# Cross-attention of a fused decoder in one pass over the scores: exponentials by queries kept, scaled, turned and copied out

## The reference

```python
q, k, v = x1 @ Wq, *split(x2 @ Wkv)              # 16 heads of 64, 256 queries, 256 keys
attn = softmax(einsum('bhid,bhjd->bhij', q, k) * 64 ** -0.5)
out = einsum('bhij,bhjd->bhid', attn, v) @ Wo + bo
```

## Time and profile before

| | |
|---|---|
| median of 3 runs | 3820.13 us (3819.62 to 3820.35) |
| span of the profiled execution | 3818.7 us |
| PE busy | 3224.1 us (84%) |
| DVE busy | 2835.6 us (74%) |
| ACT busy | 2082.8 us (55%) |
| POOL busy | 922.9 us (24%) |
| mean granted PE clock | 0.941 of full speed |

### The profile page before, as it was taken

One profiled execution on the slowest core, in us unless ns is written; L12 is line 12 of the kernel. 1 busy time (PEld: TensorE's weight loads), 2 busy tenths in 40 slices (PEclk: granted clock), 3 DMA queues, 4 the chain that ended last, 5 costly groups with the idle time before them and its releaser, 6 DMA issues.

```text
span 3818.7 us, 59008 instructions
## 1 busy us (share of the span) xinstructions
PE 3224.1 (84%) x22354; PEld 2240.1 (59%) x22402; DVE 2835.6 (74%) x4915; ACT 2082.8 (55%) x4816; POOL 922.9 (24%) x740
## 2 busy tenths in 40 slices
PE   2568989898898989989898998989889898988877
PEld 1245656666565666656566665656656565665655
DVE  4687786868778687877868778786877868687622
ACT  3356655565665656566464655656566565555432
POOL 1423050221404122140411305031230503114000
PEclk8679999999999999999999999999999999999988
DMA  5212141422304142130413213041331404123110
GB/s 187 79 61 92 31 137 47 145 70 79 128 23 148 51 136 78 55 127 33 163 51 127 87 43 138 34 158 57 114 100 31 150 34 152 62 99 109 48 42 17
DMA packets 205692, 336.50 MB, mean 88 GB/s; under 512 B 23968, under 2 KB 175008, under 8 KB 190688
## 3 DMA queue, kind: packets, MB, share of 16 engines
q1 hardware_dynamic: 205408, 332.72, 25.6%
HBM read 311.66 MB, written 20.97 MB: 87 GB/s over the span
## 4 chain that ended last, share of the span: by engine, by line
PE 55%; DVE 23%; ACT 15%; issue 6%; POOL 0%; SPq 0%; DMA 0%; DVEq 0%; ACTq 0%
PE ps L880 7%; PE ps L628 6%; PE ps L609 5%; PE ps L941 4%; DVE nm L1559 3%; PE ps L795 3%; PE ps L781 3%; PE ps L771 3%; PE ps L826 2%; ACT ps L1062 2%; PE ps L640 2%; DVE region_x L1536 2%; PE ps L553 2%; ACT region_y L1211 2%; PE ps L670 2%
## 5 line engine op out<-in xcount | busy, mean ns | idle before, releaser
L1323 POOL TENSOR_TENSOR region_x<-region_x 128x512 f32<-128x512 f32 x512 | 646.8, 1275 | 360.4 <-DVE region_x L1536 359.2
L1536 DVE TENSOR_TENSOR_SCAN region_x<-ps,region_x 128x512 f32<-128x512 f32 x512 | 614.2, 1213 | 76.4 <-ACT ps L1062 76.3
L1062 ACT ACTIVATE ps<-region_x,aneg 128x255 f32<-128x255 f32 x1024 | 440.0, 474 | 326.3 <-DVE region_x L1536 324.1
L1303 POOL TENSOR_TENSOR region_x<-region_x 128x512 f32<-128x512 f32 x96 | 121.7, 1267 | 1195.2 <-ACT region_x L1010 1190.2
L1315 POOL TENSOR_TENSOR region_x<-region_x 128x512 f32<-128x512 f32 x128 | 162.8, 1272 | 1021.4 <-DVE region_x L1516 881.2
L1559 DVE TENSOR_REDUCE nm<-ps 128x4 f32<-128x1024 f32 x256 | 308.0, 1221 | 62.5 <-PE ps L609 56.7
L880 PE MATMUL ps<-xTy,wide 128*128 128x256 f32 x1280 | 331.2, 410 | 1.1 <-DVE region_y L1723 1.1
L1211 ACT ACTIVATE region_y<-ps,rmax 128x256 f32<-128x256 f32 x512 | 235.8, 497 | 126.0 <-DVE rmax L1664 126.0
L880 PEld LDWEIGHTS ps<-xTy,wide 128*128 128x128 f32 x1280 | 251.8, 203 | 47.4 <-issue 8.7
L1664 DVE TENSOR_REDUCE rmax<-ps 128x4 f32<-128x1024 f32 x128 | 152.3, 1220 | 151.2 <-PE ps L807 151.2
L1516 DVE TENSOR_TENSOR region_x<-region_x,ps 128x512 f32<-128x512 f32 x384 | 255.0, 664 | 5.9 <-PE ps L553 5.0
(11 more groups left out here) (249 smaller groups left out, 6884.6 us busy)
## 6 DMA issues: line engine op xcount, KB each, us to landing
region_x<-rows_of_dt SPq DMA_DIRECT2D x1024, 128.0 KB, 2.9
wide<-in_wgate SPq DMA_DIRECT2D x16, 1280.0 KB, 8.2
wide<-in_wup SPq DMA_DIRECT2D x16, 1280.0 KB, 10.9
down<-in_wmoe SPq DMA_DIRECT2D x16, 1280.0 KB, 7.4
wide<-in_wq SPq DMA_DIRECT2D x16, 1024.0 KB, 5.4
wide<-in_wk SPq DMA_DIRECT2D x16, 1024.0 KB, 7.3
wide<-in_wv SPq DMA_DIRECT2D x16, 1024.0 KB, 9.6
down<-in_wo SPq DMA_DIRECT2D x16, 1024.0 KB, 12.5
```

What stands on the lines that cost most here:

```text
L1062: last = f(ps[:, 1 + 2 * (k % 2), half * T + 1:(half + 1) * T], dt_rep[k % SLOTS][:, 1:T], ACT.Exp, scale=aneg[:, k, half:half + 1])
L1323: nc.gpsimd.tensor_tensor(hbuf[k % HSLOTS], hbuf[k % HSLOTS], csb, ALU.mult).then_inc(hc_ready, 1)
L1536: nc.vector.tensor_tensor_scan(flat(hbuf[k % HSLOTS]), ps[:, 1 + 2 * (k % 2), :], flat(hbuf[k % HSLOTS]), 0.0, ALU.mult, ALU.add).then_inc ...
```

## The change

There is one pass. PE makes the scores of a pair by queries, always in banks 5 and 6. DVE takes the maximum of each head by itself. ACT takes the exponentials of a head into one of four slots `PQ`, which are kept, and their sums. DVE takes the reciprocal of the two sums and scales the head's two tiles in place. PE turns the head with four 128x128 f32 transposes into bank 7, ACT copies it into one of two slots `PT64`, and PE multiplies by the values as before. The second scores, the logarithm and the shift are gone. The orders of all four engines are new.

Names of the pieces of y below: s(u) scores of a pair, m(u) its maxima, E(u) its exponentials, S(n) the scaling of a head, T(n) its turning, C(n) its copy (with o(j): the copy of two pairs' outputs), pv(u) a pair's product with the values. Of x: l. is latent attention (l.s scores, l.m maxima, l.sT second scores, l.e exponentials, l.w weighting, l.pv values, l.o copy, l.oT, l.on, l.OT, l.On turning, scaling and copying of the result, l.wo the output projection, l.res its residual sum), win the input projection of the next sequence, conv its products, g1 to g3 the norms' estimates. The new orders of the attention stage, with x's pieces in brackets:

```diff
--- before.py
+++ after.py
@@ -38,15 +38,16 @@
 ORDER = {
-    "sp": (123, ...), "pe": (60, ...), "act": (80, ...), "v": (141, ...)
+    "sp": (140, ...), "pe": (61, ...), "act": (84, ...), "v": (145, ...)
 }
@@ -94,7 +95,7 @@
 END_STEPS = 5
 DIGIT_STEPS = 8
 DT_STEPS = 6
-Y_STEPS = 38
+Y_STEPS = 50
 A_STEPS = 5
 AY_STEPS = 3
 
@@ -152,8 +153,6 @@
         mask = sb("mask", (P, TT, T), BF16)
         VP0, VP1 = sb("VP0", (P, TT, VW)), sb("VP1", (P, TT, VW))
         nm0, nm1 = sb("nm0", (P, TT, P)), sb("nm1", (P, TT, P))
-        shiftb = sb("shiftb", (P, TT, P), BF16)
-        shiftT = sb("shiftT", (P, T), BF16)
         rmax = sb("rmax", (P, TT, 2, 8))
         rsum = sb("rsum", (P, TT, 2, 8))
         route = sb("route", (P, 5, TT, E))
@@ -212,9 +211,9 @@
         
         QT2, KT2, VV = in_y(0, (8, T)), in_y(2048, (8, T)), in_y(4096, (TT, 1024))
         OT2 = QT2
-        WSLOTS = 6
-        PT64 = in_y(6144, (WSLOTS, TT, T))
-        junk2 = in_y(6144, (8, T))
+        QSLOTS, WSLOTS = 4, 2
+        PQ = in_y(6144, (QSLOTS, TT, T))
+        PT64 = in_y(6144 + QSLOTS * TT * T, (WSLOTS, TT, T))
         mhT, sg, t1, rcmp = in_y(0, (KM, T)), in_y(2560, (2, 2, T)), in_y(3584, (2, 2, T)), in_y(4608, (2, TT, E, E))
 
         wst, wst2, hmv1 = in_y(0, (KD, FF)), in_y(2048, (KD, FF)), in_y(4096, (D,))
@@ -288,7 +287,7 @@
                     self.on_ps, self.oT = sem(tag + "_on_ps"), sem(tag + "_oT")
                 else:
                     self.kevac, self.rsum = sem(tag + "_kevac"), sem(tag + "_rsum")
-                    self.ln, self.shift = sem(tag + "_ln"), sem(tag + "_shift")
+                    self.scaled = sem(tag + "_scaled")
                 if masked:
                     self.weighed = sem(tag + "_weighed")
                 self.proj = sem(tag + "_proj")
@@ -795,40 +794,26 @@
                             last = mm(bank(b)[:, t % 2, :], wq2[:, k, t * P:(t + 1) * P], xTy[:, k, :],
                                       start=(k == 0), stop=(k == KD - 1))
                     last.then_inc(a.proj, 1)
-                yield
-                pe.wait_ge(a.evac, at(i, 4, 4))
-                for u in range(8):
-                    yield
-                    if u >= 2:
-                        pe.wait_ge(a.rsum, at(i, 8, u - 1))
+
+                def scores(u):
+                    if u:
+                        pe.wait_ge(a.rsum, at(i, 16, 2 * u))
                     for qt in range(TT):
                         for g in range(2):
                             r = slice(64 * g, 64 * g + 64)
-                            last = mm(ps[:, a.pair_bank(u) + g, qt * T:(qt + 1) * T], QT2[r, u, qt * P:(qt + 1) * P],
+                            last = mm(ps[:, 5 + g, qt * T:(qt + 1) * T], QT2[r, u, qt * P:(qt + 1) * P],
                                       KT2[r, u, :], start=True, stop=True)
                     last.then_inc(a.s_ps, 1)
-                yield
-                pe.wait_ge(a.shift, i + 1)
-                turned_shift = ps[:, 4, 0:P].bitcast(BF16)
-                for qt in range(TT):
-                    last = tr(turned_shift[:, qt * P:(qt + 1) * P], shiftb[:, qt, :], W["identb"][:])
-                last.then_inc(a.shift_ps, 1)
-                yield
-                pe.wait_ge(a.shifted, i + 1)
-
-                def scores(n):
-                    t = n // 2
-                    both = [(slice(64 * g, 64 * g + 64), a.sT_bank(n + g)) for g in range(2)]
-                    if n >= 2:
-                        pe.wait_ge(a.probs, at(i, 16, n - 1))
+
+                def turned(n):
+                    pe.wait_ge(a.scaled, at(i, 16, n + 1))
+                    if n:
+                        pe.wait_ge(a.probs, at(i, 16, n))
                     for kt in range(TT):
-                        for r, b in both:
-                            mm(ps[:, b, kt * T:(kt + 1) * T], KT2[r, t, kt * P:(kt + 1) * P], QT2[r, t, :],
-                               start=True, stop=False)
-                        for r, b in both:
-                            last = mm(ps[:, b, kt * T:(kt + 1) * T], W["selx"][r, t, :], shiftT[r, :], start=False, stop=True)
-                            if kt == TT - 1:
-                                last.then_inc(a.sT_ps, 1)
+                        for qt in range(TT):
+                            last = tr(ps[:, 7, kt * T + qt * P:kt * T + (qt + 1) * P],
+                                      PQ[:, n % QSLOTS, qt, kt * P:(kt + 1) * P], W["ident"][:])
+                    last.then_inc(a.sT_ps, 1)
 
                 def times_v(t):
                     pe.wait_ge(a.probs, at(i, 16, 2 * t + 2))
@@ -842,14 +827,23 @@
                                       start=(kt == 0), stop=(kt == TT - 1))
                     last.then_inc(a.pv, 1)
 
-                for n in range(0, 16, 2):
-                    yield
-                    scores(n)
-                    if n >= 4:
-                        yield
-                        times_v(n // 2 - 2)
-                yield
-                times_v(6)
+                yield
+                pe.wait_ge(a.evac, at(i, 4, 4))
+                scores(0)
+                for u in range(9):
+                    yield
+                    if u:
+                        turned(2 * u - 2)
+                    yield
+                    if u >= 2:
+                        times_v(u - 2)
+                    yield
+                    if u + 1 < 8:
+                        scores(u + 1)
+                    yield
+                    if u:
+                        turned(2 * u - 1)
+                yield
                 times_v(7)
                 yield
                 pe.wait_ge(down_cross, at(i, 16, 16))
@@ -1200,35 +1194,34 @@
                     act.wait_ge(a.pv, at(i, 8, 2 * j + 2))
                     f(OT2[:, 2 * j:2 * j + 2, :], bank(4), ACT.Copy).then_inc(a.o, 1)
 
-                for u in range(8):
-                    yield
+                def exps(u):
                     table(EXP_LN)
-                    act.wait_ge(a.rmax, at(i, 8, u + 1))
-                    if u >= 2:
-                        act.wait_ge(a.rsum, at(i, 8, u - 1))
-                    for qt in range(TT):
-                        for g in range(2):
-                            last = f(junk2[:, 4 * (u % 2) + 2 * qt + g], ps[:, a.pair_bank(u) + g, qt * T:(qt + 1) * T], ACT.Exp,
+                    for g in range(2):
+                        n = 2 * u + g
+                        act.wait_ge(a.rmax, at(i, 16, n + 1))
+                        if n >= QSLOTS:
+                            act.wait_ge(a.sT_ps, at(i, 16, n - QSLOTS + 1))
+                        for qt in range(TT):
+                            last = f(PQ[:, n % QSLOTS, qt, :], ps[:, 5 + g, qt * T:(qt + 1) * T], ACT.Exp,
                                      bias=rmax[:, qt, g, u:u + 1], accum_out=rsum[:, qt, g, u:u + 1])
-                    last.then_inc(a.rsum, 1)
-                yield
-                table(EXP_LN)
-                act.wait_ge(a.rsum, at(i, 8, 8))
-                f(rsum[:], rsum[:], ACT.Ln).then_inc(a.ln, 1)
-                yield
-                act.wait_ge(a.shift_ps, i + 1)
-                f(shiftT[:], ps[:, 4, 0:P].bitcast(BF16), ACT.Copy).then_inc(a.shifted, 1)
-                for n in range(16):
-                    yield
-                    table(EXP_LN)
+                        last.then_inc(a.rsum, 1)
+
+                def turned(n):
                     act.wait_ge(a.sT_ps, at(i, 16, n + 1))
-                    if n >= WSLOTS and n % 2 == 0:
+                    if n >= WSLOTS:
                         act.wait_ge(a.pv, at(i, 8, (n - WSLOTS) // 2 + 1))
-                    f(PT64[:, n % WSLOTS].rearrange("p k q -> p (k q)"), ps[:, a.sT_bank(n), :], ACT.Exp).then_inc(a.probs, 1)
-                    if n >= 9 and n % 4 == 1:
-                        output(n // 4 - 2)
-                yield
-                output(2)
+                    f(PT64[:, n % WSLOTS].rearrange("p k q -> p (k q)"), ps[:, 7, :], ACT.Copy).then_inc(a.probs, 1)
+
+                for u in range(9):
+                    yield
+                    if u < 8:
+                        exps(u)
+                    for n in (2 * u - 2, 2 * u - 1):
+                        yield
+                        if u:
+                            turned(n)
+                    if u >= 3 and u % 2 == 1:
+                        output(u // 2 - 1)
                 yield
                 output(3)
                 yield
@@ -1367,9 +1360,9 @@
             for k in range(TAPS - 1):
                 nc.vector.memset(taps[k][:, :, 0:TAPS - 1 - k], 0.0).then_inc(setup_v, 1)
             n += 3
-            for buf, value in ((VP0, 1.0), (VP1, 1.0), (nm0, 0.0), (nm1, 0.0), (shiftb, 0.0), (wsplit, 0.0)):
+            for buf, value in ((VP0, 1.0), (VP1, 1.0), (nm0, 0.0), (nm1, 0.0), (wsplit, 0.0)):
                 nc.vector.memset(buf[:], value).then_inc(setup_v, 1)
-            v.wait_ge(setup_v, n + 10)
```

(38 more changed lines are left out.)

8 lines of the change are left out of this document (4 added, 4 removed), and 19 rows, old and new, of the table ORDER.

## The result

The changed kernel takes 3938.0 us (median of 4 runs, 3927.7 to 3954.3) against 3820.2 for the kernel before on the same chip: ratio 1.0309, 95% interval [1.0289, 1.0328]. Slower was right; 3872 was not, the loss is 118 us and not 52. The profiled execution has a span of 3925.2 us, 106.5 more than in the earlier trace rows.

The account below looks back on a forecast made before the run. No engine is full over the period, so stages decide: PE's stream bounds the attention stage, which closes with a serial stretch. 15 sequences x 4 - 8 = +52 us gives 3871 profiled, 3872 as median; range 3775 to 3940.

Parts of the forecast that it names:

- the scan stage: From the MoE's end to the next cross scores: gain up to 2.2, late rows up to +1, taken as 0.
- Attention, +4: Attention stage of each sequence with a partner: +4 us, taken between PE's bound and the full walk.
- PE's work alone (+2.5): Attention stage counting only PE's added and removed work, without waits: +2.5 us a sequence.
- the walk (+5.1): Attention stage followed piece by piece through the engines' queues, each wait charged in full: +5.1 us a sequence.
- step 2: From turning the latent shift to the latent output projection: with some 3 us idle PE, projection 4.1 us later.
- Rival D: Transposes in the attention stage take a record's full 280 ns each: +9 us a sequence, 4015; chance 0.02.
- MoE, 0 (bounds -2.6 and +1): MoE: fewer ACT table changes against PE's waits at the dt projections; the pair costed at 0.
- The dt projections: Two projections now ahead of an up-projection on PE, which waits there for ACT; costed within the pair at 0.
- rival C: Gaps on PE lower its clock in the attention stage: +7 to +9 a sequence, 120 in all, 3940; chance 0.11.
- Last sequence, -8: Last sequence, without a partner, from first cross scores to wo2: -8 us, bounds -16 and 0.
- The sum: Whole kernel: 15 sequences with a partner at +4 and the last at -8, +52 us, giving 3872.

Follow-up runs that it names:

- the run at 3830: Changed kernel with SP's issue order of the kernel before put back, cross weights behind half of row 11; 3830.2 us, ratio 1.0021.
- the first run: Changed kernel with only SP's issue order put back to that of the kernel before; 3830.2 us, ratio 1.0021.
- the entry, twice: Changed kernel, self-attention's start freed: MoE's closing sum ahead of the scan's products on DVE, 3939.0 us; then ACT's copy ahead of the decays too, 3967.6 us.

## Why the prediction was wrong

*The step that failed* is the scan stage: "That gains up to 2.2 if the rows of dt are there. But SP now issues the 3 MB of cross weights between the first two rows of dt and the next, so the second product can wait for them, and the closing sum stands behind it: up to +1. I take 0." The place and the first wait are right, the size is not. The order gains 3.3 with rows on time, and the rows take 5.6 from it: 83.1 to 88.7, +2.3 against the kernel before. I priced one wait, of DVE's second product, at up to 1 us. It is 4.26 in the sequence shown; and I left out that every row behind the weights is late, so that GpSimd's second product waits too, y0 behind it, and self-attention's keys behind y0. The price stood in the trace of before, where the last rows of a sequence are issued behind the same 3 MB and wo2: a row landed 2.8 us after its issue ahead of them and 12.5 behind them (2059 to 2073.3 us, then 2075.2 to 2078.5):

```profile
region_x<-rows_of_dt SPq DMA_DIRECT2D x15, 128.0 KB, 2.8
...
region_x<-rows_of_dt SPq DMA_DIRECT2D x3, 128.0 KB, 12.5
```

The prediction named this zero as one that could fail, and the loss between the MoE's end and the self-attention scores as its sign.

*Attention, +4.* With SP's order put back it is +2.6 up to the projection, and 0 behind it. The sum is that of PE's work alone (+2.5), not of the walk (+5.1), but in part by chance: PE's bound put 1.5 ahead of the projection and 1.0 behind it. The prediction took a transpose at 0.137 us; over the run at 3830 it occupied 0.164 (168.2 / 1024). For the nine heads in step 2 that is 36 x 0.027 = 1.0 more, and with it the bound of that step comes to the measured start. PE stayed full, since other pieces of x stand between those of a head; the doubled transposes and scores show that added work of PE lengthens the stage. Behind the projection the estimate of the third norm stands where the walk put it, 10.3 us on, but the end of wo2 doesn't move.
A row of four transposes took 0.60 to 0.66 us, and a further transpose 0.123. Rival D, 0.28 each, would have shown as 18 us a sequence in the run with transposes twice, which was 6.3.
The Trainium skill (TensorE: Matmul & The Clock Gate, Part 4: PE-mode transpose) gives about 275 ns in a kernel. The trace agrees for a record's own length (288 to 292 ns) and disagrees for what it occupies.

*MoE, 0 (bounds -2.6 and +1).* It is +1.8, beyond the bound. With SP's order put back it is +1.0: PE waits 2.0 for the masks ahead of the second down product, a wait I didn't list. The dt projections, which I did list, cost 0.5. The other 0.8 in the kernel after are the low clock in half of its sequences. In four sequences the attention stage has the same step of 1.7. This is the part of rival C that came true: 11 steps, 18.6 us in all. Its figure, 3940, is next to the measured time by luck, since it put 120 us into the attention stage, which lost 3 a sequence.

*Last sequence, -8.* From s0 to the end of wo2 53.1 against 63.5: -10.4. Right, 2.4 beyond the figure and inside its bounds.

*The sum.* It took 15 like sequences. The first s0 is 6.5 later, and the sequence before the last, which runs without a partner's input projection, lost 10.9, 5.1 of it between the latent output projection and wo2: with less work of x beside it, the chain of cross-attention seems to be exposed (no run tested that). The first had no term, the second only the common +4.

*What the one pass costs.* In the orders of this change nothing in the mean period (225.4 against 225.5 with two passes and the same scan order), though its own stage is 2.6 longer. The 118 us are SP's order in this company: 108 of them by the first run, the two loads that moved in it not told apart. How much of the 108 is the rows' wait itself, and how much the way in which these periods settle on a few values, the runs don't say: one pass between old orders lost nearly as much a sequence (6.8 against 7.1) without late rows.

## What to carry to other kernels

When a change moves a large load ahead of small transfers in the same queue, price each small transfer behind it with the load's whole time, and follow each to the engine that waits in order: three engines paid here for the moved loads. Where idle time shows need not be where it is made; freeing the engine that waits (the entry, twice) didn't help or made it worse. And test a new order together with the old order of each queue: here one of the four written orders had to be put back. And when a period repeats exactly, don't read a change of a few us in one stage as won or lost before the whole period has moved.

## What the runs showed of the hardware

A DMA of 128 KB took 2.9 us from issue to landing, or 10.3 behind 3 MB issued on the same queue (12.5 behind 4 MB in the kernel before). Moving the load in the queue moved the wait: to DVE's second product, to the store and GpSimd's second product, to the product of step 8, or to GpSimd's third product.

DVE's norm with two tiles from SBUF took 0.88 us, and 1.97 while GpSimd ran its sums (shown above); a pair of scalings, with one tile, took 0.62 and 2.51. The run at 3830 shows both, with GpSimd's sums from 1778.67 on:

```profile
1776.35 0.62 DVE L1659 TENSOR_SCALAR region_y<-region_y,rsum 128x256 f32<-128x256 f32 x2
...
1778.94 2.51 DVE L1659 TENSOR_SCALAR region_y<-region_y,rsum 128x256 f32<-128x256 f32 x2
...
1783.09 0.88 DVE L1399 SCALAR_TENSOR_TENSOR region_x<-region_x,x_rstd,ln1b 128x256 f32<-128x256 f32 x2
...
1778.67 3.98 POOL L1296 TENSOR_TENSOR region_x<-region_x 128x512 f32<-128x512 f32 x3 [72.93 <-ACT region_x L1004]
```

The Trainium skill (SBUF — State Buffer, Who interferes with whom) says that DVE shares one of its SBUF port pairs with GpSimd, that an instruction of DVE with two inputs from SBUF contends there with one of GpSimd that reads SBUF, and that in DVE's two-port modes the one that comes later is blocked for the whole instruction. The rows agree that both forms get longer beside GpSimd's sums; which mode the scalings run in, no run shows.

PE's clock fell to 1.2 GHz behind thin stretches and cost 1.7 us where a dense one followed. In the kernel after PE was busy 2.13 of 4 us, and then all of 3 us at a granted 0.5 (columns as in the earlier trace rows):

```profile
828.00:832.00 4.00, 2.13 (x18) 1.51 (x15) 1.98 (x5) 4.00 (x11) 0.00 (x0) 1.00 0.02 4
832.30:835.30 3.00, 3.00 (x9) 2.38 (x8) 0.78 (x3) 1.11 (x6) 0.00 (x0) 0.50 0.00 0
```

Steady periods stood at a few values, 225.3, 228.7, 232.1 and 235.5, and gains in one stage went lost in another at 225.3 (the new scan order beside the old attention). Why these values, the runs don't settle.
